# First expert layer of a four-layer graph network: settling and router joined by chunks, rows stored by node and gathered by a place-to-node table

## The chip, the cores and the metric

The kernel runs on one core of a Trainium2 chip. The metric is the device time of one execution in microseconds (us). The engines are PE (TensorE), DVE (VectorE), ACT (ScalarE), POOL (GpSimd) and SP (SyncE, which here only issues DMA transfers). Each engine runs its own list of instructions in order, and engines wait for one another through semaphores.

## The reference, cut to what matters

N = 6250 nodes of D = 256 features pass four layers, each added to its input. The change lies in the second one and in the last step of the first.

```
x = x + _L0_gnn_ref(_layernorm(x), ...)     # softmax-weighted sum over incoming edges, 8 heads of 32
x = x + _L0_ffn_ref(_layernorm(x)[None], ...)[0]   # the first expert layer, below
x = x + _L1_gnn_ref(_layernorm(x), ...)
x = x + _L1_ffn_ref(_layernorm(x)[None], ...)[0]

def _L0_ffn_ref(x, router_w, router_b, W1, b1, W2, b2):   # E = 32 experts, H = 64
    logits = xf @ router_w.T + router_b
    idx = jnp.argmax(logits, axis=-1)                # one expert for each node
    h = relu(xf @ W1[idx] + b1[idx])
    out = relu(h @ W2[idx] + b2[idx])
```

## The kernel before

The nodes lie in NT = 49 tiles of P = 128 lanes (the last has TAIL = 106). `k.acc` holds 264 words per node in SBUF (256 features and 8 denominators), and `k.x` is its first 256 words. The stages run one after the other, and at the end of each all engines meet in a barrier and its semaphores are cleared. The names in the profile are stage and tile (`settle_x`, `moe_logits`); `nodes_acc` is `k.acc`.

- `attend0` sums the edges of the first layer. POOL issues 880 gathers (L788). SP beside it writes blanks into two tables in HBM, one pair of transfers in each of the first 49 steps (`clear`, L802): `xs0` ("sorted0", rows of the first expert layer by place) and `xs1` (of the last layer).
- `settle` divides each node's sum by its denominator (`finish`, L1149, DVE), adds the layer's input x, which SP loads in chunks of 7 tiles (L1126), on POOL (L1139), and takes DVE's statistics of the sum (L1153), all 49 tiles in a row.
- `moe0` first makes mean and 1/deviation of all 49 tiles at once (L271 to L286), and then runs the router: for each tile DVE normalises it (L228), PE transposes it (L236), ACT copies it from PSUM (L265), PE multiplies it by the router's weights (L1422), DVE adds the bias (L1383). Two buffers turn, and each engine waits for the next.
- `Route.vector` then works on [128 x 49 x 32] arrays on DVE (with 8 wide products on PE, L1281 and L1282): the best expert, and from running counts each node's **place**, so that the nodes of one expert lie together and each expert's block begins at a multiple of 128. There are 80 tiles of places.
- `send` (L1394, DVE) normalises each tile again and POOL scatters its 128 rows into `xs0` at their places by an indirect DMA (L1318), with four buffers `xi`. When all have landed, the expert loop runs.
- The expert loop takes four tiles of places a round, 20 rounds. POOL loads the next four tiles of `xs0` (L1325) when PE has transposed the ones before them (L1435); PE multiplies by W1 (L1444), DVE adds b1 (L1403), PE transposes (L1452), ACT applies relu (L1365), PE multiplies by W2 (L1457), DVE adds b2 (L1407), ACT applies relu (L1368), SP stores the tile in `ys0` (L1343). In PE's order the four transposes of round i+1 stand between the W1 products and the hidden transposes of round i.
- `attend1` gathers the results back by node (L1496). Its loop already works by chunks of 7 tiles: DVE adds (L1560), takes statistics (L1564) and normalises (L1580) in turn, with mean and 1/deviation made for one chunk at a time (L271 to L286 on 7 columns).

## Time and profile before

| | |
|---|---|
| median of 3 runs | 3166.9 us (3164.47 to 3168.32) |
| the profiled execution | 3159.72 us, its span 3158.1 us |
| PE busy | 2201.9 us (70%) |
| DVE busy | 1782.5 us (56%) |
| POOL busy | 1590.8 us (50%) |
| ACT busy | 1326.0 us (42%) |
| granted TensorE clock, mean | 0.806 |

The spans in the rows are those of the profiled execution. Times in rows are from the start of its span. In a row of the timeline the first number is the start, the second how long the piece lasts, x how many instructions it holds, and the bracket how long the engine sat idle before it and what released it. PEclk is the granted TensorE clock: 0.50 is 1.2 GHz and 1.00 is 2.4 GHz.

### The profile page before, as it was taken

How to read it: one execution, taken by the hardware profiler on the slowest of the kernel's cores; microseconds unless marked ns; L12 is line 12 of the kernel's file. 1: busy time of each engine (PE TensorE's matmuls, PEld its weight loads, DVE VectorE, ACT ScalarE, POOL GpSimd, SP SyncE). 2: the span in 40 equal slices, each digit the busy share in tenths (PEclk: the TensorE clock that was granted, in tenths of full speed). 3: DMA queues.
4: the chain of work that ended last, by engine and by line, in shares of the span. 5: the costliest groups of instructions: out<-in, count | busy, mean ns of one | idle time of the engine just before them, and what ended most of it. 6: DMA issues, size and time to landing. Idle time of an engine off the chain costs nothing. (4 is left out here: it accounts for less than half of the span.)

```text
span 3158.1 us, 49641 instructions
## 1 busy us (share of the span) xinstructions
PE 2201.9 (70%) x13093; PEld 1863.9 (59%) x13094; DVE 1782.5 (56%) x4090; ACT 1326.0 (42%) x2973; POOL 1590.8 (50%) x1585
## 2 busy tenths in 40 slices
PE   7999966777777777777628069620700099999998
PEld 6888855565666555565517057410700088888887
DVE  2411026777777777776585524656753456556564
ACT  3444445555655555565402025310211444444443
POOL 0047337777777777777450443657047033333433
PEclk8999977888888888887765569765555599999999
DMA  6456466777765555555724135632212622222331
GB/s 187 152 194 232 186 220 200 210 211 205 213 178 144 145 145 143 143 145 131 73 83 119 53 118 176 144 66 51 83 61 101 235 42 47 49 47 45 48 50 24
DMA packets 213447, 402.41 MB, mean 127 GB/s; under 512 B 46139, under 2 KB 141096, under 8 KB 206639
## 3 DMA queue, kind: packets, MB, share of 16 engines
q0 software_dynamic: 84864, 206.63, 27.9%
q1 hardware_dynamic: 127278, 193.40, 18.8%
q8 instruction: 59, 0.97, 0.1%
q10 hardware_dynamic: 1168, 0.79, 0.1%
q14 instruction: 78, 0.63, 0.1%
HBM read 247.26 MB, written 155.68 MB: 128 GB/s over the span
## 5 line engine op out<-in xcount | busy, mean ns | idle before, releaser
L788 POOL DMA_INDIRECT sum_ring<-h_tab,gnn_edge_row x880 | 840.3, 955 | 267.9 <-issue 260.6
L1049 PE MATMUL sum_bank<-sum_ring,sum_one_hot 128*128 128x264 f32 x1760 | 580.7, 494 | 208.8 <-issue 191.7
L1049 PEld LDWEIGHTS sum_bank<-sum_ring,sum_one_hot 128*128 128x128 f32 x1760 | 418.1, 247 | 327.1 <-issue 222.5
L1875 POOL DMA_INDIRECT out_dram<-moe_y,moe_to_node x112 | 186.6, 1666 | 383.1 <-ACT moe_y L1901 352.1
L699 PE MATMUL rows_bank<-rows_w_rows,rows_xnT 128*128 128x264 f32 x1568 | 363.0, 391 | 6.8 <-ACT rows_h_rows L495 6.7
L699 PEld LDWEIGHTS rows_bank<-rows_w_rows,rows_xnT 128*128 128x128 f32 x1568 | 298.1, 193 | 56.7 <-ACT rows_h_rows L495 7.6
L838 ACT ACTIVATE sum_distance_by_lane<-all_iota,gnn_minus_local 128x128 bf16<-128x128 f32 x880 | 267.4, 386 | 0.1
L904 DVE TENSOR_TENSOR sum_ring<-sum_ring,sum_bank 128x1024 f32<-128x1024 f32 x220 | 265.7, 1209 | 0.4 <-ACT sum_ring L852 0.4
L1038 PEld LDWEIGHTS sum_bank<-gnn_dst_half,sum_one_hot_T 128*128 128x128 f32 x1760 | 229.9, 208 | 42.8 <-issue 39.3
L1038 PE MATMUL sum_bank<-gnn_dst_half,sum_one_hot_T 128*128 x1760 | 235.0, 292 | 27.1 <-ACT sum_one_hot_T L831 14.4
L2033 PE MATMUL moe_bank<-moe_w_low,moe_hidden_high 128*128 x896 | 244.4, 273 | 0.0
L2033 PE MATMUL moe_bank<-moe_w_high,moe_hidden_low 128*128 x896 | 244.3, 273 | 0.0
L2033 PE MATMUL moe_bank<-moe_w_high,moe_hidden_high 128*128 x896 | 244.3, 273 | 0.0
L495 ACT ACTIVATE rows_h_rows<-rows_bank 128x264 f32<-128x264 f32 x392 | 152.3, 390 | 210.2 <-PE rows_bank L699 195.9
L911 DVE TENSOR_TENSOR nodes_acc<-sum_bank,nodes_acc 128x264 f32 x440 | 188.2, 428 | 50.5 <-PE sum_bank L1049 20.1
L1917 ACT ACTIVATE moe_hidden<-moe_bank,moe_b_T 128x256 f32<-128x256 f32 x456 | 186.2, 475 | 39.5 <-PE moe_bank L2023 21.6
L843 ACT ACTIVATE sum_one_hot<-sum_distance_by_lane,all_ones 128x1024 f32<-128x1024 bf16 x110 | 126.3, 1149 | 142.8 <-PE sum_bank L1049 140.9
L596 DVE COPY gnn_dst_half<-rows_bank 128x64 f32<-128x64 f32 x49 | 11.0, 225 | 295.6 <-PE rows_bank L704 295.6
L2023 PE MATMUL moe_bank<-moe_x_high,moe_w_high 128*128 128x256 f16 x912 | 174.9, 274 | 1.7 <-DVE moe_x_low L1967 1.7
L894 DVE TENSOR_TENSOR sum_score<-sum_dst_part,sum_ring 128x64 f32<-128x64 f32 x110 | 24.8, 226 | 267.5 <-DMA sum_ring<-h_tab,gnn_edge_row 266.9
L2023 PE MATMUL moe_bank<-moe_x_low,moe_w_high 128*128 128x256 f16 x912 | 175.0, 274 | 0.0
L2023 PE MATMUL moe_bank<-moe_x_high,moe_w_low 128*128 128x256 f16 x912 | 174.9, 274 | 0.0
(408 smaller groups left out, 4164.2 us busy)
## 6 DMA issues: line engine op xcount, KB each, us to landing
h_tab<-rows_h_rows SPq DMA_DIRECT2D x49, 1056.0 KB, 3.9
sum_local_rows<-local_tab SPq DMA_DIRECT2D x110, 256.0 KB, 3.8
sorted<-sum_blank_row SPq DMA_DIRECT2D x49, 387.0 KB
moe_stage<-in_L_ffn_W_dram SPq DMA_DIRECT2D x16, 1024.0 KB
moe_tile<-sorted POOLq DMA_DIRECT2D x58, 258.0 KB, 4.2
sum_ring<-h_tab,gnn_edge_row POOLq DMA_INDIRECT x880, 3.8
sorted<-sum_zero SPq DMA_DIRECT2D x49, 256.0 KB
mask_tab<-rows_masks POOLq DMA_DIRECT2D x7, 1560.0 KB, 7.2
```

Of the source, the lines that this page charges most:

```text
L495: nc.scalar.activation(hb[:, t % 2, r, :], bank[2 + r % 4][:, 0:W0], ACT.Copy).then_inc(h_ok.sem, 1)
L699: last = nc.tensor.matmul(bank[2 + r % 4][:, 0:W0], norm.xT[:, u, c * P:(c + 1) * P], wx[:, c, r, :], start=(c == 0), stop=(c == DC - 1))
L788: nc.gpsimd.indirect_dma_start(ring[:, t % (RING * ST), :], None, k.h_tab, bass.IndirectOffsetOnAxis(k.edge_row[:, t:t + 1], 0)).then_inc( ...
L838: last = nc.scalar.activation(off[:, u * P:(u + 1) * P], k.iota[:, :], ACT.Abs, bias=k.minus_local[:, m * ST + u:m * ST + u + 1])
L904: nc.vector.tensor_tensor(to, to, by, ALU.mult).then_inc(msg_ok, 1)
L911: nc.vector.tensor_tensor(col(k.acc, b), sum_b[g % SG][:, 0:W0], col(k.acc, b), ALU.add).then_inc(added, 1)
L1038: last = nc.tensor.matmul(pick_b[n % 2][:, u * R * H0:(u + 1) * R * H0], hotT[:, n % 2, u, :], col(k.dst_half, b[u // G]), start=True, sto ...
L1049: last = nc.tensor.matmul(sum_b[j][:, 0:W0], hot[:, m % 2, t, :], ring[:, m % RING * ST + t, :], start=(u == 0), stop=(u == G - 1))
L1875: nc.gpsimd.indirect_dma_start(a["out"], bass.IndirectOffsetOnAxis(to_node[:, n % 2, h:h + 1], 0), y[:, n % 2, h, :], None, bounds_check=N ...
L1917: last = nc.scalar.activation(hg[:, q, m * B1:(m + 1) * B1], bank[q][:, m * B1:(m + 1) * B1], ACT.Gelu, scale=1.0 / (XS * WS), bias=col(b1 ...
L2023: last = nc.tensor.matmul(bank[q][:, m * B1:(m + 1) * B1], w1[pw][:, c, bass.ds(e * F1 + (2 * q + m) * P, P)], xh[px][:, u, c, :], start=( ...
L2033: last = nc.tensor.matmul(bank[6 + u][:, h * D:(h + 1) * D], hh[ph][:, u, m, h * P:(h + 1) * P], w2[pw][:, m, bass.ds(e * D, D)], start=(m ...
```

## The change

`settle` is gone as a stage. `moe0` begins with a loop over 7 chunks of 7 tiles: while a chunk is normalised and goes through the router, DVE and POOL finish the next chunk and take its statistics, and mean and 1/deviation are made for 7 columns. x is loaded four chunks ahead, into the tile that later holds b2. The normalised tiles lie in a ring of XN = 8, from which PE transposes them and SP stores them by node in a table in HBM, `xn0` ("normal0"), whose first 128 rows are zero. The weights are loaded by ACT's queue (router, W1, b1) and SP's (W2 in the third chunk, b2 after the last addition).

There is no second normalisation and no scatter. After the places are known, `slots` builds on DVE, for four node tiles at a time, two one-hot arrays: `hot_lane` (is the node's place in this lane of its tile of places) and `hot_tile` (is it in this tile of places, times the node's row number in `xn0`). PE adds their 49 products in one PSUM bank, which makes the table `slot_rows`: for each of 84 tiles of places and each lane the row of `xn0` that lies there, 0 (a zero row) where the place is empty. POOL then gathers the 84 tiles of the expert loop by that table, where it loaded them in one piece before. In `attend0` the blanks for `xs0` are no longer written.

```diff
 def attend0(nc, a, k):
...
             def clear(t):
-                for (tab, m), empty, w in zip(k.sorted, (zero, blank), (D, XW)):
+                for (tab, m), empty, w in zip(k.sorted, (blank,), (XW,)):
...
             sp.wait_ge(zero_ok, 4)
+            sp.dma_start(k.xn0[0:P, :], zero[:, :]).then_inc(zeroed, 16)
...
-def settle(nc, a, k):
...
+    def slots(self, v, ch):
...
+        for b, step in enumerate(self.steps):
+            if b >= 2:
+                v.wait_ge(self.hot_used, b - 1)
+            m, q0 = len(step), step[0]
+            nc.vector.tensor_tensor(self.hot_lane[:, b % 2, 0:m, :], self.k.iota[:, :].rearrange("p (o l) -> p o l", o=1).broadcast_to([P, m, P]),
+                                    self.lane[:, q0:q0 + m].rearrange("p (m o) -> p m o", o=1).broadcast_to([P, m, P]), ALU.is_equal)
+            for q in step:
+                last = nc.vector.tensor_scalar(self.hot_tile[:, b % 2, q - q0, :], self.starts[:, :], self.first[:, q:q + 1], self.code[:, q:q + 1], ALU.is_equal, ALU.mult)
+            last.then_inc(self.hot_ok, 1)
+        v.wait_ge(self.hot_used, len(self.steps))
+        nc.vector.tensor_scalar(self.rows[:, :], self.bank[0][:, 0:self.starts.shape[1]], 0.25, None, ALU.add).then_inc(self.rows_ok, 1)
...
+    def slot_rows(self, pe):
...
+                last = self.nc.tensor.matmul(self.bank[0][:, 0:self.starts.shape[1]], self.hot_lane[:, b % 2, q - step[0], :], self.hot_tile[:, b % 2, q - step[0], :],
+                                             start=(q == 0), stop=(q == n - 1))
...
 def moe0(nc, a, k):
...
         def _(pool):
             route.pool()
-
             for t in range(NT):
-                u, m = t % 4, P if t < NT - 1 else TAIL
-                pool.wait_ge(row_ok, t + 1)
-                nc.gpsimd.indirect_dma_start(k.xs0, bass.IndirectOffsetOnAxis(k.rows0[0:m, t:t + 1], 0), xi[0:m, u, :], None).then_inc(scattered[u], 16)
...
+                nc.gpsimd.tensor_tensor(k.x[:, t, :], k.x[:, t, :], x[:, n % AHEAD, u, :], ALU.add).then_inc(node_ok, 1)
+            all_written(pool)
+            pool.wait_ge(route.rows_ok, 1)
+            for n in range(T + 4):
+                x_ps.slot(pool, n)
+                nc.gpsimd.indirect_dma_start(xi[:, n % 4, :], None, k.xn0, bass.IndirectOffsetOnAxis(tile_rows[:, n:n + 1], 0)).then_inc(tile_in[n % 4], 16)
...
         def _(sp):
...
+            for c in range(CHUNKS):
+                if c + AHEAD < CHUNKS:
+                    sp.wait_ge(node_ok, (c + 1) * CH)
+                    load_x(c + AHEAD)
+                if c == 2:
+                    sp.dma_start(w2[:, :, :], a["L0_ffn_W2"].rearrange("e h d -> h e d")).then_inc(loaded_b, 16)
+                for t in range(c * CH, (c + 1) * CH):
+                    sp.wait_ge(xn_ok, t + 1)
+                    sp.dma_start(k.xn0[(t + 1) * P:(t + 2) * P, :], xn[:, t % XN, :]).then_inc(written[t % XN], 16)
+            sp.wait_ge(node_ok, NT)
...
         def _(v):
...
+            def normalise(t):
+                if t >= XN:
+                    v.wait_ge(t_ps, t - XN + 1)
+                    v.wait_ge(written[t % XN], 16 * (t // XN))
...
+            for c in range(CHUNKS):
...
+                if more:
+                    finish(t1 + LEAD)
+                    stats(t1)
+                scales(c)
+                for j in range(CH):
+                    normalise(t0 + j)
+                    if more and j + 1 < CH:
+                        finish(t1 + j + 1 + LEAD)
+                        stats(t1 + j + 1)
+                    if j == 2 and c:
+                        logits(c - 1)
+                if more:
+                    variance(c + 1)
+            route.codes(v, ch)
...
             route.vector(v, ch)
+            route.slots(v, ch)
...
-            def send(i, u):
...
-            rounds(v, NT, 4, send)
```

On POOL the order around the first expert layer reads as follows, before (-) and after (+); `sorted` is `xs0`, `normal` is `xn0`, `moe_b` in the addition is the b2 tile that holds x.

```order
-L1133 MEMSET settle_x 128x256
-L1139 TENSOR_TENSOR nodes_acc<-nodes_acc,settle_x 128x256 x49
-L112 UNCONDITIONAL_BRANCH
-L115 ISA
-L1311 UNCONDITIONAL_BRANCH
-L1211 IOTA moe_tile_row_i 1x80
-L1318 DMA sorted<-moe_tile,nodes_rows 12544x256 x49
...
+L1155 IOTA moe_tile_row_i 1x80
+L1331 TENSOR_TENSOR nodes_acc<-nodes_acc,moe_b 128x256 x49
+L1336 DMA moe_tiles<-normal,moe_slot_rows 128x256 x84
```

The 49 scatters are gone, and the loads of the loop (one direct transfer for each tile) have become 84 gathers.

On DVE the end of one chunk and the start of the next read in the changed kernel as follows (`moe_work` holds the denominators, `moe_tiles` the ring of normalised tiles).

```order
L1435 TENSOR_SCALAR moe_tiles<-nodes_acc,moe_mean,moe_rstd 128x256
L271 TENSOR_TENSOR moe_tmp<-nodes_stats 128x7
L272 TENSOR_SCALAR moe_mean<-moe_tmp 128x7
...
L277 SCALAR_TENSOR_TENSOR moe_var<-moe_var,moe_tmp 128x7
L1414 TENSOR_TENSOR nodes_acc<-nodes_acc,moe_work 128x256
L1418 BN_STATS nodes_stats<-nodes_acc 128x6
L282 RECIPROCAL moe_rstd<-moe_sd 128x7
...
L286 TENSOR_TENSOR moe_rstd<-moe_rstd,moe_tmp 128x7
L1435 TENSOR_SCALAR moe_tiles<-nodes_acc,moe_mean,moe_rstd 128x256
L1414 TENSOR_TENSOR nodes_acc<-nodes_acc,moe_work 128x256
```

The settling of the next chunk now stands between the normalisations of this one, where it was a stage of its own.

On DVE the end of the places reads in the changed kernel as follows; `moe_total` and `moe_running` are the memory of `hot_lane` and `hot_tile`.

```order
L1217 CAST moe_expert<-moe_expert_f 1x80
L1254 CAST moe_place_i<-moe_place 128x49
L1255 TENSOR_SCALAR moe_place_i<-moe_place_i 128x49
L1256 CAST moe_tile_of<-moe_place_i 128x49
L1259 TENSOR_TENSOR moe_lane_of<-moe_place,moe_tile_of 128x49
L1264 TENSOR_TENSOR moe_total<-all_iota,moe_lane_of 128x512
L1267 TENSOR_SCALAR moe_running<-moe_tile_starts,moe_tile_of,moe_row_code 128x84 x4
...
L1270 TENSOR_SCALAR moe_slot_rows<-moe_bank 128x84
L1473 CAST nodes_rows<-moe_place 128x49
```

The pair L1264, L1267 stands there 13 times (the last time for one tile); before, the cast to `nodes_rows` came straight after `moe_expert`, and then 49 normalisations for the scatter.

## Rows read from the trace of the kernel before
**Rows 1.** Stretch: busy (x) of PE, PEld, DVE, ACT, POOL; PEclk, DMA share, GB/s

```profile
1606.40:1655.10 48.70, 0.00 (x0) 0.00 (x0) 44.90 (x100) 0.01 (x1) 41.43 (x50) 0.53 0.42 132
1655.10:1725.40 70.30, 63.19 (x296) 59.48 (x296) 33.10 (x113) 20.28 (x51) 0.18 (x1) 0.50 0.52 135
1725.40:1773.20 47.80, 7.08 (x16) 3.75 (x16) 38.98 (x38) 0.00 (x0) 0.00 (x0) 0.57 0.00 0
1773.20:1842.20 69.00, 0.00 (x0) 0.00 (x0) 19.99 (x49) 0.00 (x0) 48.08 (x49) 0.50 0.26 93
1842.20:1978.30 136.10, 119.38 (x728) 101.25 (x728) 49.91 (x160) 71.42 (x244) 45.22 (x84) 0.88 0.51 158
```

**Rows 2.** Timeline of the stretch of settle, POOL and DVE

```profile
1612.00 35.94 POOL L1139 TENSOR_TENSOR nodes_acc<-nodes_acc,settle_x 128x256 f32<-128x256 f32 x42 [5.27 <-DMA settle_x<-in_x_dram]
...
1616.54 0.60 DVE L1149 TENSOR_TENSOR nodes_acc<-nodes_acc,settle_denominator 128x256 f32<-128x256 f32 x1
...
1617.40 0.60 DVE L1149 TENSOR_TENSOR nodes_acc<-nodes_acc,settle_denominator 128x256 f32<-128x256 f32 x1
```

**Rows 3.** Timeline of DVE in the router loop, and its end

```profile
1717.42 0.41 DVE L228 TENSOR_SCALAR moe_y<-nodes_acc,moe_mean,moe_rstd 128x256 f32 x1 [0.43 <-PE moe_bank L236]
...
1720.06 0.41 DVE L228 TENSOR_SCALAR moe_y<-nodes_acc,moe_mean,moe_rstd 128x256 f32 x1 [0.43 <-PE moe_bank L236]
...
1725.14 0.19 DVE L1383 TENSOR_TENSOR moe_logits<-moe_bank,moe_router_bias 128x32 f32<-128x32 f32 x1 [0.66 <-PE moe_bank L1422]
```

**Rows 4.** Timeline of DVE where the places are made, wide array, end

```profile
1727.41 1.79 DVE L1222 TENSOR_TENSOR moe_work<-moe_logits,moe_best 128x1568 f32<-128x1568 f32 x1
...
1772.93 0.19 DVE L1387 CAST nodes_rows<-moe_place 128x49 int32<-128x49 f32 x1
```

**Rows 5.** Timeline of POOL and PE at the loop's first loads

```profile
1842.24 2.59 POOL L1325 DMA_DIRECT2D moe_tile<-sorted  x4 [5.56 <-DMA sorted<-moe_tile,nodes_rows]
...
1844.52 2.82 PE L1435 MATMUL moe_bank<-all_ident,moe_tile 128*128 128x128 f32 x8 [101.18 <-DMA moe_tile<-sorted]
```

**Rows 6.** Timeline of DVE in attend1, the start of a chunk

```profile
2019.38 0.20 DVE L282 RECIPROCAL gnn_rstd<-gnn_sd 128x7 f32<-128x7 f32 x1 [1.06 <-ACT gnn_sd L1529]
...
2020.68 0.41 DVE L1580 TENSOR_SCALAR gnn_xn<-nodes_acc,gnn_mean,gnn_rstd 128x256 f32<-128x256 f32 x1
2021.01 0.42 DVE L1560 TENSOR_TENSOR nodes_acc<-nodes_acc,gnn_expert_rows 128x256 f32<-128x256 f32 x1
```

**Rows 7.** Timeline of ACT in attend1, the square root that opens each chunk

```profile
2008.27 0.20 ACT L1529 ACTIVATE gnn_sd<-gnn_var 128x7 f32<-128x7 f32 x1
2019.14 0.20 ACT L1529 ACTIVATE gnn_sd<-gnn_var 128x7 f32<-128x7 f32 x1
2031.91 0.20 ACT L1529 ACTIVATE gnn_sd<-gnn_var 128x7 f32<-128x7 f32 x1
```

**Rows 8.** Timeline of the expert loop: transposes of two rounds, loads between

```profile
1882.98 1.04 PE L1435 MATMUL moe_bank<-all_ident,moe_tile 128*128 128x128 f32 x8
...
1884.02 2.55 POOL L1325 DMA_DIRECT2D moe_tile<-sorted  x4 [3.21 <-PE moe_bank L1435]
...
1888.73 1.04 PE L1435 MATMUL moe_bank<-all_ident,moe_tile 128*128 128x128 f32 x8
```

**Rows 9.** Landing times by the DMA view, in KB each and us

```profile
moe_tile<-sorted POOLq DMA_DIRECT2D x84, 128.0 KB, 2.4
...
gnn_expert_rows<-results,nodes_rows POOLq DMA_INDIRECT x49, 3.8
```

**Rows 10.** Landing of attend0's 880 gathers (L788), from the view of their line

```profile
DMA to landing us min/median/max: 2.7/3.8/5.8
```

**Rows 11.** As rows 1: attend0 while blanks are written, and later

```profile
800.00:900.00 100.00, 76.74 (x344) 60.87 (x345) 76.10 (x157) 54.44 (x109) 75.63 (x81) 0.81 0.70 202
1000.00:1100.00 100.00, 77.85 (x360) 61.56 (x360) 75.48 (x156) 56.40 (x111) 75.75 (x80) 0.83 0.52 144
```

**Rows 12.** As rows 1: the expert loop in its first 27 us

```profile
1845.00:1872.00 27.00, 26.69 (x101) 22.26 (x101) 6.09 (x20) 9.94 (x30) 6.45 (x12) 0.50 0.35 107
```

More of the change, by code:

```diff
@@ L1283, in tensor, with slots_in @@
         last.then_inc(self.counted, 1)
+    def slots_in(self, s, tiles, hot_lane, hot_tile, rows):
+        n = self.top * NT
+        self.lane, self.first, self.code = (s.sb(x, [P, n]) for x in ("lane_of", "tile_of", "row_code"))
+        self.place_i, self.starts = s.sb("place_i", [P, n], I32), s.sb("tile_starts", [P, tiles])
+        self.hot_lane, self.hot_tile, self.rows = hot_lane, hot_tile, rows
+        self.hot_ok, self.hot_used, self.rows_ok = s.sem("slots_ready"), s.sem("slots_used"), s.sem("slot_rows_ready")
+        self.steps = [range(q, min(q + 4, n)) for q in range(0, n, 4)]
@@ L1309, in moe0, with all_written @@
         block = s.block()
+        def all_written(eng):
+            for u in range(XN):
+                eng.wait_ge(written[u], 16 * ((NT - u + XN - 1) // XN))
         @block.gpsimd
@@ L1348, in _ @@
         def _(act):
-            norm.root(act)
-            tiles(act, NT, 2, lambda t, u: norm.keep(act, t, u, lg_ps))
+            act.dma_start(rw_n[:, :], a["L0_ffn_router_w"]).then_inc(router, 16)
+            act.dma_start(rb[:, :], a["L0_ffn_router_b"].rearrange("(o e) -> o e", o=1).broadcast_to([P, E0])).then_inc(router, 16)
+            for c in range(DC):
+                act.dma_start(w1[:, c, :, :], a["L0_ffn_W1"][:, c * P:(c + 1) * P, :].rearrange("e p h -> p e h")).then_inc(loaded, 16)
+            v = a["L0_ffn_b1"].rearrange("e h -> (e h)").rearrange("(o n) -> o n", o=1)
+            act.dma_start(flat(b1[:, :, :]), v.broadcast_to([P, v.shape[1]])).then_inc(loaded, 16)
+            for c in range(CHUNKS):
+                part = slice(c * CH, (c + 1) * CH)
+                act.wait_ge(var_ok, c + 1)
+                nc.scalar.activation(sd[:, part], var[:, part], ACT.Sqrt).then_inc(sd_ok, 1)
+                for t in range(c * CH, (c + 1) * CH):
+                    act.wait_ge(t_ps, t + 1)
+                    if t >= 2:
+                        act.wait_ge(lg_ps, t - 1)
+                    nc.scalar.activation(xnT[:, t % 2, :], bank[t % 2][:, 0:D], ACT.Copy).then_inc(t_ok, 1)
             act.wait_ge(route_ok, 1)
```

218 lines of the change are left out of this document (122 added, 96 removed).

## The prediction

> **What bounds the kernel now.** I read the busy times by stretch first, because the shares of the whole span mix stages. From the end of attend0 at 1606.4 to the start of attend1 at 1978.3 no engine is the bound of the whole; one after the other is [rows 1]. In settle POOL and DVE are both busy and PE stands still for 48.7 us. In the router loop PE is (63.2 of 70.3 us, at the lower clock, 0.50). Making the places is a chain on DVE, 47.8 us. In the 69.0 us of the scatter PE does nothing at all and POOL issues 49 transfers. In the expert loop PE is the bound again (119.4 of 136.1 us). The stretches follow one another, so a microsecond taken from any of them is one off the time, unless the next one gives it back.
>
> The timelines then give the pace. In settle DVE's pair of division and statistics repeats every 0.86 us (1616.54 to 1617.40), and so do POOL's additions (42 in 35.94 us) [rows 2]. Two tiles of the router take 2.64 us, 1.32 each, and its last logits come at 1725.3 [rows 3]. The places end at 1773.1 [rows 4]; PE's first transpose of the expert loop starts at 1844.5 [rows 5]: 71.4 us between them.
>
> **Joined loop, -22 us.** Before: 1606.4 to 1725.3, 118.9 us. After, in steps:
> - Head. The first addition starts at 1612.0, as before, since it waits for the first chunk of x [rows 2]. Seven tiles at 0.86 us, then statistics: 1618.5. Moments are 7 small operations at about 0.20 us, the duration of such a one [rows 6]: 1.4. One pair (0.86), the router's copy (0.2), and the five steps to 1/deviation, 1.3 us in attend1 (2019.38 to 2020.68) [rows 6]. First normalisation at 1622.3.
> - One chunk. Seven pairs at 0.86, seven normalisations at 0.33 (the pace 2020.68 to 2021.01) [rows 2, 6], 1.4 and 1.3 for the small ones, 0.3 for logits: 11.3 us. attend1, which has the same form, takes 10.9 and 12.8 us a chunk (2008.27, 2019.14, 2031.91) [rows 7]. I take 11.6, near the sum: attend1's POOL issues gathers where this one adds. Six chunks: 1691.9.
> - Last chunk. Nothing is settled beside it, so PE bounds it: seven tiles at 1.32 [rows 3] and two more of such turns until the first is through, 12 at most; I take 11.3. Logits at 1703.2.
> That is 96.8 us against 118.9. Bounds: 11.3 a chunk gives 2 us more; 12.8 takes 7. A first chunk of x that comes late, since four chunks and ACT's weight loads start with it, costs up to 5.
>
> What hides here: PE needs 7 x 1.32 = 9.2 us a chunk, under 11.3. SP's stores of the ring (128 KB each) are waited for eight tiles later, some 12 us, against a landing of 2.4 us for such a size [rows 9]; W2 issued in the third chunk delays them, up to 3 us. The loads of x, the weights and the stores are about 18 MB in 97 us, 185 GB/s, which attend0 moves (202) [rows 11]. The 4 MB of b2 leave after the last addition and have some 75 us of places and table; at 202 GB/s they take 20. The small operations of `codes` lie under PE's last chunk.
>
> The trace shows DVE and POOL in each other's way: the division takes 0.60 us in settle [rows 2], a two-input operation of the same size 0.42 where POOL only gathers [rows 6]. By the Trainium skill ("SBUF — State Buffer", Who interferes with whom) VectorE and GpSimd share a port pair: a VectorE operation with two SBUF inputs contends with GpSimd's reads, and one in a 2-port mode blocks it. By that rule the normalisation, a tensor-scalar operation, could take part too and would hold POOL's additions up. The row has it at 0.41 us for 256 columns, like the two-input one, so it runs in no such mode here; I leave it at 0.33 in the sum and keep the other case as a rival.
>
> **Places, 0.** The same instructions stand there, with the same 8 products.
>
> **Table instead of scatter, -47 us.** Before, 71.4 us from the places to PE's first transpose [rows 4, 5]. After:
> - Four small operations, 0.8 us.
> - 12 full steps and one single. On DVE one of 512 columns and four of 84. A wide operation of 1568 columns takes 1.79 [rows 4], so 512 take 0.6; one of 49 columns takes 0.19 [rows 4], and without a wait behind it at least 0.13, so four of them take 0.5 to 0.8. On PE four products, which the router does in 1.32 at the lower clock (two of 128 and two of 32 columns) [rows 3]. The buffers are doubled, so the slower counts: 1.4 a step, 17 us. The bounds are 1.1 a step (13.5 us) and 2.0 (24.5 us), if the handing over is not hidden.
> - Emptying PSUM and waking POOL, 1.3 us. Table ready at 19 us; bounds 15.5 and 27.
> - The first gather lands. No row shows one from `xn0`; gathers of rows of about this size take 2.7 at least and 3.8 in the median [rows 9, 10], a direct load started at 1842.24 feeds PE at 1844.52 [rows 5]. I take 3.3 with the wait.
> - Gathers leave POOL every 1.25 us (80 in 100 us) [rows 11] where four loads take 2.59 [rows 5]: the fourth tile is 1.7 us later.
> 24.0 us against 71.4.
>
> **Expert loop, +11 us.** A round is 5.75 us at the full clock (1882.98 to 1888.73), its transposes take 1.04, and POOL's first load starts 1.04 after the first of them [rows 8]. POOL's fourth gather starts 1.04 + 3 x 1.25 = 4.8 us after the transposes' start and lands at 4.8 + L; it is due at 5.75 + 0.78 = 6.5. What is missing, L - 1.7, is shared by two rounds, because a round that stalls also starts the next later: (L - 1.7)/2 a round. With L = 2.7 that is 0.5, with 3.8 it is 1.05. Loads in this very loop land in 2.4 [rows 9], 0.1 above the idle one, so I take L = 3.0, 0.65 a round. About 17 of the 20 rounds run at the full clock; in the first 27 us only three do, at 0.50 [rows 12], and there nothing is missing. Together 11 us, bounds 8 and 18. Behind the stalled transposes PE's hidden transposes and W2 products queue, and DVE, ACT and SP behind these, so all of it is on the path. By the Trainium skill ("DMA: Bandwidth & Descriptors", Anatomy of one DMA) such a transfer takes 2.0 us and its bytes at 436 GB/s, 2.3 us for 128 KB; the loop would then lose 5 us and not 11. No row has a gather that fast.
>
> **attend0, 0.** 49 transfers of 256 KB less. But POOL issues 80 or 81 gathers in 100 us while blanks are written and 80 afterwards, at 202 and 144 GB/s [rows 11]: the issue is the bound, and DMA was hidden. Price 0; a few fewer late landings could give 2.
>
> **Sum.** -22 - 47.4 + 11 = -58.4. The profiled execution took 3159.7 us (span 3158.1), which is 7.2 below the median of the runs, 3166.9. 3159.7 - 58.4 = 3101.3 for an execution like it, and **3108 us** on the scale of the medians. Less than 0.2% (6 us) can't be told from no change here.
>
> **The rivals.**
> 1. *POOL bounds the expert loop* (0.15). The gathers land like attend0's slowest, 5.8 us [rows 10], because 42% of their rows are the one zero row (4502 empty of 10752) and all read the same address. (5.8 - 1.7)/2 = 2.05 a round, 35 us: 3132. For it: POOL would be busy 5.0 of 5.75 us. Against: the median of 3.8.
> 2. *The joined loop is paced by the shared port or by DMA* (0.12). If each normalisation costs 0.2 more and each addition holds DVE up, a chunk takes 13.5 to 14 us: +13, 3121. For it: the 0.60 against 0.42. This is the skill's rule on ports from above, in a milder form.
> 3. *PE's clock is up when the loop starts* (0.11). Before, PE stood still for 101 us ahead of it and ran 27 us at 0.50; now it works through the table's products until some 5 us before. Three rounds at 5.75 in place of 9 give 10: 3098; with the last chunk at the higher clock too, 3094.
> 4. *Slower* (0.02). The table and the gathers would have to lose the 69 us won. That is a landing of gathers of L = (69/17) x 2 + 1.7 = 9.8 us, far above the largest of 5.8. With L = 10.5 it is 75 us lost: 3173.
> 5. *Nothing gained* (0.01): the loop waits for something else that is late, b2 above all, until the old time. It would have to land 50 us after my estimate.
>
> **How the numbers follow.** The likeliest case has 0.59, with its own range 3096 to 3122 (head and chunks +12 or -2, table +8 or -4, loop +7 or -3, not all at once). The range over the cases, 3092 to 3134, leaves out rival 4 and the far ends, some 2 in 10 with what I have not thought of. Faster: all but rivals 4 and 5 and a margin, 0.95; same 0.02; slower 0.03.
>
> **What the profile will show.** The last logits 97 us after the end of attend0, with chunks of 11 to 12 us, divisions at 0.5 to 0.6; 13 steps at 1.4 us; the first gather some 68 us after the last logits; rounds of 6.2 to 6.6 us at the full clock with PE's transposes waiting for the fourth gather, POOL almost without idle time; the pace of attend0 unchanged. I would be wrong through the chunk (waits of DVE on stores or on the square root), through the step of the table, or through a landing time unlike 3 us.

## Result and profile after the change

The changed kernel takes 3144.6 us in the median of nine runs (3132.8 to 3158.1); the kernel before took 3166.9 in the runs beside them (3152.5 to 3168.3). The ratio is 0.994, with a 95% interval of 0.9925 to 0.9956: 0.6% faster. The forecast was 3108 with a range of 3092 to 3134; the sign was right and the size was not. The profiled execution has a span of 3141.1 us, 17.0 less than before, where 58.4 were forecast. One execution of e7 (3562.6 us) and one of e17 (3270.9 us) were over 1.5% above the fastest of their kernel and are left out of its median and ratio.

The stretches of the stage in the changed kernel (columns as in [rows 1]; in order: the head, the joined loop to its last normalisation, the router's last tiles, the places, the table, the expert loop):

```profile
1606.40:1630.40 24.00, 0.42 (x2) 0.28 (x2) 14.13 (x34) 2.06 (x4) 8.81 (x12) 0.56 1.01 267
1630.40:1706.60 76.20, 58.12 (x261) 53.15 (x261) 65.61 (x206) 17.99 (x50) 27.51 (x38) 0.50 0.54 147
1706.60:1714.00 7.40, 6.90 (x35) 6.76 (x35) 1.94 (x8) 1.92 (x5) 0.00 (x0) 0.50 0.93 366
1714.00:1761.90 47.90, 7.37 (x16) 3.90 (x16) 38.85 (x38) 0.00 (x0) 0.00 (x0) 0.57 0.10 44
1761.90:1788.50 26.60, 22.68 (x98) 21.35 (x98) 21.09 (x68) 0.00 (x0) 0.00 (x0) 0.50 0.00 0
1791.30:1960.90 169.60, 145.04 (x728) 119.81 (x728) 50.52 (x160) 75.26 (x244) 77.36 (x83) 0.75 0.51 126
```

attend0 ends where it did (1606.3, before 1606.4), though it moves less (153 GB/s over its length instead of 164): its term of 0 was right. The last logits come at 1714.0 instead of 1703.2, and the places take 47.9 us as before. PE's first transpose starts 29.4 us after the places (forecast 22.3, before 71.4). The expert loop takes 169.6 us with a mean clock of 0.75, where [rows 1] has 0.88 over the old one. From first transpose to the start of attend1 it was 133.8 before, so the loop gives 35.8 us back and not 12.7 (11 for its rounds and 1.7 for the spacing of its first gathers).

**The head.** ACT at the stage's start:

```profile
1607.57 0.88 ACTq L1374 DMA_DIRECT2D moe_w<-in_L_ffn_W_dram  x1
1608.48 0.40 ACT L1374 MOVE_SHAPE moe_w<-in_L_ffn_W_dram  x1 [0.94 <-issue]
1608.91 10.04 ACTq L1374 DMA_DIRECT2D moe_w<-in_L_ffn_W_dram  x1
1618.98 8.83 ACTq L1376 DMA_DIRECT2D moe_b<-in_L_ffn_b_dram  x1
1627.84 1.28 ACT L1380 ACT_TABLE_LOAD   x1 [18.96 <-issue]
1629.13 0.21 ACT L1380 ACTIVATE moe_sd<-moe_var 128x7 f32<-128x7 f32 x1
```

The second half of W1 and b1 hold ACT for 10.0 and 8.8 us each: this is the issue of a DMA, not its landing. The square root that the first chunk needs, with its table load of 1.3 us, stands behind them. DVE had the variances at 1620.8 and soon idled for 7.4 us, until the square root was done at 1629.3; the first normalisation starts at 1630.4, not 1622.3.

**The chunks** are 11.55 us apart (1630.42, 1641.97, 1653.54, 1665.08), as forecast, but of other parts. DVE in the fourth:

```profile
1665.08 0.41 DVE L1435 TENSOR_SCALAR moe_tiles<-nodes_acc,moe_mean,moe_rstd 128x256 f32<-128x256 f32 x1
1665.40 0.42 DVE L1414 TENSOR_TENSOR nodes_acc<-nodes_acc,moe_work 128x256 f32<-128x256 f32 x1
1665.74 0.42 DVE L1418 BATCH_NORM_STATS2 nodes_stats<-nodes_acc 128x6 f32<-128x256 f32 x1
1672.16 0.41 DVE L1435 TENSOR_SCALAR moe_tiles<-nodes_acc,moe_mean,moe_rstd 128x256 f32<-128x256 f32 x1 [6.00 <-DMA normal<-moe_tiles]
...
1673.16 0.70 DVE L1435 TENSOR_SCALAR moe_tiles<-nodes_acc,moe_mean,moe_rstd 128x256 f32<-128x256 f32 x1
```

The division takes 0.42 and not 0.60, the normalisation mostly 0.69 and not 0.41: POOL's addition now runs beside the normalisation, where in [rows 2] it ran beside the division. And once DVE waits 6.0 us for a store of the ring: this store was issued at 1654.0, behind W2 (1652.45), and took 18.1 us to land where the median is 1.8.

**The table.** DVE's wide comparison of two steps in turn, 3.72 us apart, 1.86 a step against the 1.4 forecast:

```profile
1766.54 0.69 DVE L1264 TENSOR_TENSOR moe_total<-all_iota,moe_lane_of 128x512 f32<-128x512 f32 x1 [0.56 <-PE moe_bank L1278]
1767.15 1.02 DVE L1267 TENSOR_SCALAR moe_running<-moe_tile_starts,moe_tile_of,moe_row_code 128x84 f32<-128x84 f32 x4
...
1770.26 0.69 DVE L1264 TENSOR_TENSOR moe_total<-all_iota,moe_lane_of 128x512 f32<-128x512 f32 x1 [0.39 <-PE moe_bank L1278]
```

DVE has some 1.6 us of work in a step (1.54 in e17 below, where it does not wait) and then waits for PE. PE at the lower clock, first in the table and then in the router of the kernel before:

```profile
1764.49 7.95 PE L1278 MATMUL moe_bank<-moe_running,moe_total 128*128 128x84 f32 x33 [32.20 <-DVE moe_running L1267]
```

```profile
1716.45 0.67 PE L236 MATMUL moe_bank<-all_ident,moe_y 128*128 128x128 f32 x2
1716.91 0.90 PE L1422 MATMUL moe_bank<-moe_router,moe_y 128*128 128x32 f32 x4
```

A product is two instructions on PE, a transpose is one. So a step of the table has eight, 98 in all for the 49 products, and a tile of the router has six.

**The expert loop.** PE in two rounds, and the landing of the 84 gathers from the view of their line:

```profile
1821.05 2.00 PE L1541 MATMUL moe_bank<-moe_w,moe_tiles 128*128 x16
1822.88 0.93 PE L1532 MATMUL moe_bank<-all_ident,moe_tiles 128*128 128x128 f32 x6
1825.11 0.41 PE L1532 MATMUL moe_bank<-all_ident,moe_tiles 128*128 128x128 f32 x2 [1.29 <-DMA moe_tiles<-normal,moe_slot_rows]
...
1828.76 3.67 PE L1541 MATMUL moe_bank<-moe_w,moe_tiles 128*128 x16
1832.23 1.91 PE L1532 MATMUL moe_bank<-all_ident,moe_tiles 128*128 128x128 f32 x8
```

```profile
DMA to landing us min/median/max: 2.7/3.4/6.3
```

PE waits for the fourth gather, as forecast. What was not forecast is the next round: W1's products take 3.67 us instead of 2.00, the clock is at 0.50. That comes back six times. The same 728 instructions keep PE busy 145.0 us, 25.6 more than before, and this is most of the 35.8; only 10 us are longer stands.

### The profile page after: what moved, and what is told of

It is laid out like the page before. It is cut to its first block and busy times, and to the rows that moved or that the text cites. A ratio compares the mean times of both kernels' runs of the same rounds, so it can differ in the third digit from the quotient of the medians.

```text
span 3141.1 us, 48982 instructions
## 1 busy us (share of the span) xinstructions
PE 2252.2 (72%) x13191; PEld 1907.5 (61%) x13192; DVE 1791.8 (57%) x4143; ACT 1331.6 (42%) x2981; POOL 1570.9 (50%) x1535
## 5 line engine op out<-in xcount | busy, mean ns | idle before, releaser
L788 POOL DMA_INDIRECT sum_ring<-h_tab,gnn_edge_row x880 | 838.6, 953 | 268.0 <-issue 259.4
L912 DVE TENSOR_TENSOR nodes_acc<-sum_bank,nodes_acc 128x264 f32 x440 | 188.5, 428 | 56.2 <-PE sum_bank L1050 26.6
```

The costliest lines, as they stand in the source:

```text
L788: nc.gpsimd.indirect_dma_start(ring[:, t % (RING * ST), :], None, k.h_tab, bass.IndirectOffsetOnAxis(k.edge_row[:, t:t + 1], 0)).then_inc( ...
L912: nc.vector.tensor_tensor(col(k.acc, b), sum_b[g % SG][:, 0:W0], col(k.acc, b), ALU.add).then_inc(added, 1)
```

## Experiments

Each group ran on a chip of its own, with the kernel before beside it. On the chips of the first four groups the kernel before takes 3494 to 3571 us instead of 3164 to 3167. Nearly all of the difference lies in attend0 (its 100 us from 800 hold 64 gathers in the trace of the second group where [rows 11] have 81). So I compare ratios within a group, and stages by their traces. All times from the stage's start, in us; the loop is from PE's first transpose to the start of attend1. The ratio is that of the timed runs to the kernel before in the same group (a 95% interval of 0.002 to 0.007 to either side); where there is none, the kernel ran once, for its trace.

| run | group | last logits | first transpose | loop | attend1 starts | clock in loop | ratio |
|---|---|---|---|---|---|---|---|
| before | | 118.9 | 238.1 | 133.8 | 371.9 | 0.88 | |
| changed | | 107.7 | 185.0 | 169.6 | 354.6 | 0.75 | 0.994 |
| c1, c2 (changed again) | 2, 3 | 108.4, 108.2 | 185.7, 185.2 | 171.8, 175.4 | 357.5, 360.6 | 0.74, 0.70 | 0.989, 0.994 |
| e3 weights late | 1 | 94.4 | 172.1 | 163.0 | 335.1 | 0.80 | 0.988 |
| e4 eight tiles | 1 | 109.0 | 185.6 | 161.6 | 347.2 | 0.76 | 0.988 |
| e5 direct loads | 1 | 106.8 | 184.0 | 138.5 | 322.5 | 0.85 | |
| e6 fill | 1 | 107.9 | 185.2 | 172.3 | 357.5 | 0.84 | 0.991 |
| e7 spread | 2 | 108.1 | 185.7 | 147.5 | 333.2 | 0.89 | 0.984 |
| e8, e12 all | 2, 3 | 94.4, 94.4 | 171.5, 171.4 | 164.9, 157.8 | 336.4, 329.2 | 0.74, 0.77 | 0.985, 0.986 |
| e9 stall | 2 | 108.1 | 184.8 | 132.5 | 317.3 | 0.90 | |
| e13, e14 stalls | 4 | 107.4, 107.9 | 184.4, 184.5 | 139.6, 162.4 | 324.0, 346.9 | 0.88, 0.73 | |
| e15 node order | 4 | 107.6 | 185.0 | 155.0 | 340.0 | 0.83 | |
| e11 add on DVE | 3 | 114.4 | 191.7 | 171.2 | 362.9 | 0.75 | |
| e10, e18 late and spread | 3, 5 | 94.5, 94.4 | 172.2, 171.7 | 152.6, 148.0 | 324.8, 319.7 | 0.82, 0.86 | 0.981, 0.982 |
| e16, e17 warm | 4, 5 | 94.3, 94.4 | 169.5, 169.4 | 140.6, 137.4 | 310.1, 306.8 | 0.96, 0.96 | 0.985, 0.978 |

The changed kernel was not run in groups 1, 4 and 5. In group 2 the times alone do not tell e7 (0.979 to 0.988) from the changed kernel (c1, 0.985 to 0.992); there, and for e3, the gain is read from the traces.

### The weights' place (e3)

My theory was that the issue of W1 and W2 holds up whoever issues next on that queue; the rival, that the chunks of x fill the queues anyway.

```diff
 # ACT
-            for c in range(DC):
-                act.dma_start(w1[:, c, :, :], ...).then_inc(loaded, 16)
-            act.dma_start(flat(b1[:, :, :]), ...).then_inc(loaded, 16)
             for c in range(CHUNKS):
...
+            for c in range(DC):
+                act.dma_start(w1[:, c, :, :], ...).then_inc(loaded, 16)
+            act.dma_start(flat(b1[:, :, :]), ...).then_inc(loaded, 16)
             act.wait_ge(route_ok, 1)
 # SP
-                if c == 2:
-                    sp.dma_start(w2[:, :, :], ...).then_inc(loaded_b, 16)
...
             sp.wait_ge(node_ok, NT)
+            sp.dma_start(w2[:, :, :], ...).then_inc(loaded_b, 16)
```

> W1 and b1 are issued by ACT after its last copy of the router loop, W2 by SP after the last addition, ahead of b2. Theory A (a full DMA queue holds up whoever issues into it: ACT's square root behind W1 and b1, DVE's normalisation behind the stores that SP could not start after W2): the first normalisation comes at 1622.3 instead of 1630.4, the wait of 6.0 us on a store is gone, chunks stay at 11.55, the last logits come near 1700 instead of 1714, and the time falls by 14 us. Rival B (the four chunks of x and the stores fill the queues by themselves): the first normalisation stays near 1630 or the 6 us reappear elsewhere, the time falls by under 4. Rival C: the 9 MB of weights then land after the table is ready and the loop starts late: the loop's first transpose stays near 1791.

The first normalisation comes at 16.5 instead of 24.1, the last logits at 94.4 instead of 107.7, and the loop's first transpose 12.9 us earlier, so the weights, 5 MB of them moved and 9 MB in all, land in time behind the places and the table. DVE's waits over the joined loop, in the changed kernel and then in this one:

```profile
DVE moe_rstd L282 <- ACT moe_sd L1380: 9.0, 2, 7.4
DVE moe_tiles L1435 <- DMA normal<-moe_tiles: 6.0, 1, 6.0
DVE moe_logits L1439 <- PE moe_bank L1512: 5.1, 1, 5.1
```

```profile
DVE moe_logits L1438 <- PE moe_bank L1511: 5.2, 1, 5.2
DVE moe_rstd L282 <- ACT moe_sd L1375: 1.6, 1, 1.6
```

Both waits are gone and nothing took their place. That the issues held up the square root and the store is shown; theory A's sum of 14 us was 13.3. Its picture of a full queue is not: here the issue of W1's second half takes 20.9 us, with no chunk of x under way but behind W2 and b2, and nothing that the stage waits for stands behind it.

### What the loop waits for (e5, e7, e15)

e5 replaces the gathers by direct loads of the same table in node order (the tiles are then not sorted by expert):

```diff
-nc.gpsimd.indirect_dma_start(xi[:, n % 4, :], None, k.xn0, bass.IndirectOffsetOnAxis(tile_rows[:, n:n + 1], 0))
+pool.dma_start(xi[:, n % 4, :], rows(k.xn0, (n % NT + 1) * P, P))
```

> The 84 gathers of the expert loop are direct loads of 128 rows of the same table in node order (so the tiles are not sorted by expert; everything else is done). Theory A (the gathers are what the loop lost by): rounds of 5.75 us with the clock at 1.00 after some 27 us, loop 133 to 138 us instead of 169.6, time 32 to 36 less. Rival B (the loop is slow by what is around it, weights or stores): the loop stays over 160.

At the full clock 14 of its 16 rounds take 5.75 or 5.76 us, and PE never waits for a tile after the first ones. So the gathers are what the loop lost by; the changed kernel itself takes 171.8 and 175.4 on chips of this kind. e7 keeps them and changes which row an empty place reads:

```diff
-nc.vector.tensor_scalar(self.rows[:, :], self.bank[0][...], 0.25, None, ALU.add)
+nc.vector.tensor_scalar(self.rows[:, :], self.bank[0][...], 0.25, self.k.col[:, 0:1], ALU.add, ALU.max)
```

Empty places hold 0, and nodes' rows start at 128, so the maximum with the lane's number sends lane p of an empty place to zero row p.

> Empty places are coded with the lane instead of 0, so that they read 128 different zero rows and not all the same one; nothing else differs. If the one hot row makes gathers slow (the first rival of the prediction), the gathers land earlier by over 0.5 us in the median and the loop falls from 170 to 150 or less. If it does not, landings stay near 3.4 us and the loop stays within 5 us of the changed kernel's in the same group.

The loop took 147.5 us against 171.8 for the changed kernel in the same group, 24.3 less, and PE's waits for gathers are 9.7 us in all against 18.8. Once the clock is up it stays up to the loop's end, as it does in e10 and e18, which have this edit too. Of the landing I had no reading on that chip; the fifth group has one, in e18:

```profile
L1336 POOL DMA_INDIRECT moe_tiles<-normal,moe_slot_rows x84: 940/946/964, 1770.9 to 1910.5; - x84
...
DMA to landing us min/median/max: 2.8/3.1/3.2
```

The largest is 3.2 us, where it was 6.3, and the median 3.1 against 3.4. The one zero row was what made gathers late. e15 gathers by a table in node order, with no empty places at all (again unsorted tiles):

> The loop still gathers, by indirect DMA, but the table holds the rows in node order (row 128 x tile + lane, none empty, none twice in a tile), so the tiles are not sorted. If the hot zero row is the whole reason why gathers land late, the waits on gathers are those of the run with spread zero rows (0.5 us a round) and the loop takes 145 to 150. If the scattered order of rows costs time too, waits are shorter than that, 0 to 0.3 a round. If neither, the loop stays near 170.

PE's waits for gathers are 8.9 us in all, near e7's 9.7, and its rounds 6.3 to 6.8 as e7's 6.3 to 6.8. So the order in which the rows lie costs nothing that shows. Its loop is longer than e7's (155.0) because it begins with four rounds at 0.50 where e7 has two.

### Why the clock falls (e6, e9, e13, e14)

Count a round from the start of W1's products to the next, and as stand all the time in it in which PE does nothing. In the five traces of the four-buffer loop with one zero row (changed, c1, c2, e3, e11), 16 rounds have 2 us or more of stand. All 16 have a fall to 0.50 in them. Below 2 us it goes either way: the first trace has three falls in rounds with 1.3, 1.7 and 1.8 us of stand, and the largest stand without a fall is 1.7 (c1). That is a correlation, so I made stands of known size on direct loads. The edit is the direct load of e5, and ahead of the fourth load of every fourth round:

```diff
+                if n % 16 == 15:
+                    pool.wait_ge(spare_ok, n // 16)
+                    nc.gpsimd.tensor_tensor(spare[:, 0:1024], mask[:, 0:1024], mask[:, 0:1024], ALU.add).then_inc(spare_ok, 1)
                 pool.dma_start(xi[:, n % 4, :], ...)
```

> Direct loads in node order as in the earlier run (tiles not sorted), and in every fourth round one addition of 1024 columns on POOL ahead of the fourth load, which makes this load some 1 to 2 us late for PE; five such stalls in the loop. Theory A (a stall of this length brings the granted clock to 0.50): each stall is followed by a round at 0.50, which costs 2 to 4 us beyond the stall itself, the loop takes 152 to 168 us instead of 138.5. Rival B (the clock is not brought down by stalls): only the stalls are added, 5 to 8 us, the loop takes 144 to 147 us and the clock stays at 1.00 between them.

The addition took 1.9 us and the stand was only 0.4: too short to be a test. The clock did not fall with it, and the loop (132.5) was shorter than e5's by luck: its clock was up 9 us after the loop's start, e5's after 37, and no run gives a reason for that. So the doses were raised.

> As the run with a stall (direct loads in node order, tiles not sorted; POOL adds ahead of the fourth load in every fourth round), but the addition has 1536 columns in place of 1024, 2.85 us instead of 1.90, so that PE should stand some 1.4 us instead of 0.4, five times. If stalls of that length bring the clock down, each is followed by a round at 0.50 and the loop takes 150 to 160 us against 132.5 to 138.5; if not, it takes 138 to 145.

> The same with two additions of 1024 columns, 3.8 us, so that PE should stand some 2.3 us, five times. In the runs of the changed kernel nearly every round with 1.7 us or more of stand at the full clock had a fall to 0.50 in it. If the stand is the cause, all five stalls do that and the loop takes 158 to 168 us; if the falls come by themselves, the stalls cost 2.3 us each and the loop takes 144 to 150.

With stands of 0.9 to 1.2 us (1.3 to 1.6 in the whole round, where an undisturbed one has 0.5) a fall came in one round of five, and the loop took 139.6. With 1.9 to 2.1 us (2.3 to 2.5 in all) all three that met the full clock brought a fall; the other two met a clock that was down already. The loop took 162.4. The first of the three:

```profile
2172.52 2.00 PE L1546 MATMUL moe_bank<-moe_w,moe_tiles 128*128 x16
2174.36 0.82 PE L1537 MATMUL moe_bank<-all_ident,moe_tiles 128*128 128x128 f32 x6
2177.11 0.41 PE L1537 MATMUL moe_bank<-all_ident,moe_tiles 128*128 128x128 f32 x2 [1.93 <-DMA moe_tiles<-normal]
...
2178.33 3.29 PE L1559 MATMUL moe_bank<-moe_w,moe_hidden_T 64*128 x8 [0.37 <-ACT moe_hidden_T L1405]
2181.55 3.67 PE L1546 MATMUL moe_bank<-moe_w,moe_tiles 128*128 x16
```

A stand of 1.93 us, with 0.37 more behind it, and then three whole rounds and parts of two at 0.50: these five rounds take 46.8 us and not 28.8. That stands of this size bring the clock down in this loop is shown. That they are the only cause is not: e5, e9, e13 and e14 have one fall each with no such stand ahead of it, and c1 and c2 one each with 0.5 and 0.9 us.

e6 tried the reverse, work for PE in place of the stand: six transposes into a bank that is overwritten, ahead of the wait for the fourth gather.

```diff
+                    if u == 3:
+                        for r in range(6):
+                            nc.tensor.transpose(bank[7][:, D:D + P], k.ident[:, :], k.ident[:, :])
                     turn(i + 1, u)
```

> Work is added: six more transposes of 128 columns on PE in each round, ahead of the wait for the fourth gather (120 in all, 0.13 us each at the full clock, 0.27 at half; their result is overwritten). Theory A (the stand of PE brings the clock down): PE works where it stood, the clock stays at 1.00 after the first rounds, rounds take 6.2 to 6.8, and the loop is shorter than 169.6 in spite of the added work: about 140 to 150, time 20 to 30 less. Rival B (the clock falls for another reason): the loop gets longer by 5 to 25 us.

The mean clock is 0.84, where the changed kernel has 0.70 to 0.75, but the loop took 172.3, as long as there (169.6 to 175.4): the 120 transposes cost what the clock gave. Neither theory's numbers came. It is no clean test either: the clock still falls five times in the loop, and the added work brings new stands of up to 1.5 us ahead of W2's products.

### More buffers (e4, e8, e12)

Four more tile buffers in memory that is dead by then (`route.pick`), PE's loop unrolled to two rounds, and POOL waiting for the tile eight places back:

```diff
+        xb = flat(route.pick[0][:, :, :])[:, 0:4 * D].rearrange("p (u f) -> p u f", u=4)
+        xi = [xa[:, u, :] for u in range(4)] + [xb[:, u, :] for u in range(4)]
...
-                x_ps.slot(pool, n)
+                if n >= 8:
+                    pool.wait_ge(x_ps.sem, n - 3)
```

> The expert loop has eight tile buffers instead of four, so that POOL gathers one round further ahead. Theory A (late fourth gathers make PE stand still for 0.3 to 1.3 us, and each such stand is followed by a round at a granted clock of 0.50): PE never waits for a gather after the first rounds, the clock stays at 1.00 after some 27 us, rounds take 5.75, the loop takes 133 to 138 us instead of 169.6 and the time falls by 32 to 36. Rival B (the clock falls for another reason, or POOL's 5.0 us a round are the bound): the waits of about 22 us go, but slow rounds at 0.50 remain; the loop takes 150 to 160 and the time falls by 10 to 20.

The waits for gathers went (5.6 us in all, the first tiles), as both theories said, and the loop is 161.6: rival B. e8 adds late weights and spread rows, and e12 is e8 again.

> W1, b1 and W2 late as in the run with the weights late, eight tile buffers as in the run with eight tiles, and empty places read 128 different zero rows instead of one. Theory A (stalls on gathers bring the clock down): the loop's first transpose comes 172 us after the stage's start and on an undisturbed chip the loop takes 133 to 140 us, the time is 45 to 50 us under the changed kernel. Rival B (with deeper gathers something else stalls PE, as DVE's waits on stores in the run with eight tiles): the loop stays near 160, the time is 20 to 25 us under it.

> The kernel with all three edits (weights late, eight tile buffers, spread zero rows) once more, to see if its loop of 164.9 us, with two long stretches at the lower clock and no stall ahead of them, comes again. If such stretches come by chance, the loop takes 140 to 150 us this time; if eight buffers bring them, it stays at 160 to 168.

164.9 and 157.8. In all three the clock falls two to four times, with at most 0.8 us of stand in the round of the fall and in the one ahead of it. From e12:

```profile
2096.67 1.05 PE L1534 MATMUL moe_bank<-all_ident,moe_tiles 128*128 128x128 f32 x8
2097.64 0.98 PE L1552 MATMUL moe_bank<-all_ident,moe_hidden 128*128 128x128 f32 x4
2099.13 1.99 PE L1557 MATMUL moe_bank<-moe_w,moe_hidden_T 64*128 x8 [0.51 <-issue]
2101.05 3.50 PE L1544 MATMUL moe_bank<-moe_w,moe_tiles 128*128 x16
```

What does differ from e5 is that the hidden transposes are stretched (0.98 us, in e5 0.60), since DVE begins its additions 2.6 us after the start of W1's products, not 1.2. Why the clock falls there stays open, and eight buffers were not run on a chip like the first and the last.

### The port (e11)

The additions of x made by DVE, not POOL:

```diff
-                nc.gpsimd.tensor_tensor(k.x[:, t, :], k.x[:, t, :], x[:, n % AHEAD, u, :], ALU.add).then_inc(node_ok, 1)
...
+                nc.vector.tensor_tensor(k.x[:, t, :], k.x[:, t, :], x[:, n % AHEAD, u, :], ALU.add).then_inc(node_ok, 1)
```

> The 49 additions of x are made by DVE instead of POOL. If POOL's additions are what makes DVE's normalisation take 0.69 us instead of 0.41 in the changed kernel (a shared port), all 49 normalisations now take 0.41, at a pace of 0.33, and a chunk takes 7 x 4 x 0.34 + 3.0 = 12.5 us instead of 11.55. If the 0.69 has another cause (the stores that read the ring, PE's reads), it stays and a chunk takes 14 us or more.

DVE's 49 normalisations, in the changed kernel and in this one (ns, least/median/most):

```profile
L1435 DVE TENSOR_SCALAR moe_tiles<-nodes_acc,moe_mean,moe_rstd x49: 390/692/764, 1630.4 to 1706.3; 128x256 f32<-128x256 f32 x49
```

```profile
L1434 DVE TENSOR_SCALAR moe_tiles<-nodes_acc,moe_mean,moe_rstd x49: 396/398/413, 1909.4 to 1991.7; 128x256 f32<-128x256 f32 x49
```

POOL's addition is the cause of the 0.69. That is the rule of the Trainium skill ("SBUF — State Buffer", Who interferes with whom) which the prediction set aside; the trace agrees with it in that the normalisation is long beside POOL's addition and short without it. Whether it runs in a 2-port mode, the trace does not show. Without POOL the joined loop is still 6.2 us longer than c2's, about 1 us for each of six chunks, since DVE has a fourth operation per tile.

### Versions (e10, e16, e17, e18), and the references

> The changed kernel once more, as the reference of this group, because the chip of the first group ran the kernel before in 3559 us instead of 3167. Every theory expects the stages of the first result: 107.7 us to the last logits, the loop's first transpose at 185, and a loop of 170 us with the clock falling to 0.50 several times; on a chip like that of the first group also delays of DVE and ACT while gathers run, which the first result does not show.

> The changed kernel, as the reference of this group. Every theory expects 107.7 us to the last logits, the loop's first transpose at 185 and a loop of 168 to 173 us.

The ratios to the kernel before are 0.9888 (0.9851 to 0.9924) and 0.9935 (0.9914 to 0.9955).

> W1, b1 and W2 late, and empty places spread over the 128 zero rows, four tile buffers as in the changed kernel. If the two causes found so far (the DMA queues ahead of ACT's square root and of DVE's ring, 14 us; the hot zero row, 24 us) are independent, the loop's first transpose comes at 172, the loop takes 145 to 150 us, and the time is 35 to 40 us under the changed kernel's in the same group. If the loop of the spread run was short by luck of the clock, the loop is over 160.

3421.5 us against 3473.1 for c2: 51.6 less, a ratio to before of 0.9805 (0.9776 to 0.9834). In the traces the stage is 35.8 us shorter (324.8 against 360.6), as expected. The traced executions differ outside it too, by 18.8 us ahead of the stage and by 11 behind it, where the kernels are the same; so not all of the 51.6 is shown to be the edits' work. e16 is this kernel with work for PE ahead of the loop:

```diff
 # slot_rows, in each step
+            for r in range(2):
+                self.nc.tensor.transpose(self.bank[7][:, 256:384], self.k.ident[:, :], self.k.ident[:, :])
 # ahead of the first turn
+            for r in range(24):
+                nc.tensor.transpose(bank[7][:, D:D + P], k.ident[:, :], k.ident[:, :])
```

> The best kernel so far (weights late, zero rows spread), and PE given work in the wait ahead of the loop: two transposes of 128 columns more in each of the table's 13 steps, and 24 more before the first gather has landed (results overwritten). If PE's clock at the start of the loop follows what PE did before, the first three to four rounds of 9.9 us take 6.3 instead and the time falls by a further 10 to 16 us, to 0.976 to 0.978 of the kernel before. If the clock rises no sooner, the time stays at 0.98.

The clock came up in the table, fell for 7 us in the loop's first round, behind stands for the first gathers, and is at 1.00 from the second round on. The ratio, 0.9852 (0.9803 to 0.9902), was too wide to tell it from e10, so the two ran side by side:

> The kernel with late weights, spread zero rows and added work for PE ahead of the loop, beside the same one without the added work. If the clock that is up at the start of the loop is worth its 12 us (loop 140.6 us against 152.6 in the traces of two groups), this one is 0.3 to 0.4% faster than the other in the same group, at 0.977 of the kernel before. If the work added makes the clock fall later in the loop, both are equal.

> The kernel with late weights and spread zero rows, as the partner of the one with added work: 0.980 of the kernel before as in its first group, with three to four rounds of 9.9 us at the start of the loop and a loop of 150 to 155 us.

e17 takes 3093.1 us, 0.9778 of before (0.9760 to 0.9795), e18 3106.0, 0.9816 (0.9796 to 0.9836); the kernel before took 3164.3. The loop of e18, then that of e17:

```profile
1773.70:1921.70 148.00, 126.96 (x728) 104.59 (x728) 50.24 (x160) 73.82 (x244) 77.23 (x83) 0.86 0.47 145
```

```profile
1782.00:1919.40 137.40, 113.21 (x728) 93.32 (x728) 49.96 (x160) 72.77 (x244) 77.01 (x82) 0.96 0.50 155
```

The same 728 instructions take 113.2 us where they took 127.0. In e18 the clock is at 0.50 for the loop's first 39.5 us and then does not fall again. In e17 it is up from 1762.3, falls once, at 1786.2, behind four stands of 0.4 to 0.8 us for the first gathers, is back at 1793.0 and stays up. And the step of the table shrinks from 1.86 to 1.54 us, DVE's own work, since PE's products now run at the full clock for most of it. e17 is the fastest kernel here: 2.2% under the kernel before, against 0.6% for the change as made.

## Why the prediction was wrong, step by step

The terms, as times of the stage; "repaired" is e18, which differs from the changed kernel in two things, where the weights are issued and which zero row an empty place reads.

| term | forecast | changed | repaired |
|---|---|---|---|
| joined loop | -22.0 | -11.2 | -24.5 |
| places | 0 | +0.1 | 0 |
| table and first gather | -49.1 | -42.0 | -41.9 |
| expert loop (with 1.7 of spacing) | +12.7 | +35.8 | +14.2 |
| attend0 | 0 | -0.1 | |
| sum | -58.4 | -17.4 | -52.2 |

- **Head (8.1 us short).** The step that failed: "First normalisation at 1622.3". The landing of x was weighed ("costs up to 5"), and x did land as before. What I did not cost is that the issue itself holds the engine: ACT 18.9 us, with the square root behind it. I asked what stands behind a wait and not what stands behind an issue. e3 shows it. The trace of before had the sign of it, in SP's issues of W1 and W2 at the start of `moe0`, where nothing stood behind them:

```profile
1656.07 4.81 SPq L1334 DMA_DIRECT2D moe_w<-in_L_ffn_W_dram  x2
1660.93 4.87 SPq L1335 DMA_DIRECT2D moe_w<-in_L_ffn_W_dram  x1
```

- **Chunks (right in sum by luck, wrong in parts) and W2.** 11.55 against 11.6. The pair of division and statistics fell from 0.86 to 0.67, and the normalisation rose from 0.33 to 0.62: POOL's addition lengthens whichever of the two it meets. The duration of 0.41 where POOL only gathers could not show that the normalisation is immune, because that row had no POOL addition beside it; e11 shows it. Rival 2 was priced from this and its mechanism is real, but its chunk of 13.5 to 14 did not come, since what the division gave paid for it. "W2 ... delays them, up to 3 us" measured 6.0; a last chunk of 9.9 instead of 11.3 and smaller differences took back 3.2.
- **Places and attend0.** Right, with the work that hides the blanks (POOL's issue) as named.
- **Table (7.1 short).** The step was mis-sized: 1.86 us and not 1.4. DVE's part is 1.54 (the four operations of 84 columns take 0.94 in it, above my 0.5 to 0.8), and a step of PE at the lower clock takes 1.86, not 1.32. I read it off the router as four products of 128 and 32 columns. But two of those four are transposes, one instruction each, and a product is two: six instructions there and eight here, which at 0.50 follow one another about every 0.21 us with 32 columns as with 84; the rest of the 1.86 is handing over. That is 5.5 us over twelve steps; the end of the table and the first gather took another 1.6.
- **Expert loop (23.1 short, the largest miss).** The step that failed is one landing time for every gather and rounds "at the full clock" whatever PE waits. "I take L = 3.0, 0.65 a round" was right for a gather without the hot row: e18 has 3.1 and rounds of 6.2 to 6.4, and its loop is 1.5 us off the forecast. Rival 1 named the hot row, and I gave it 0.15 because the median of attend0's gathers, which have no such row, speaks against it; those rows could not bear on it. The rival also had the wrong form: not every gather at 5.8, but a median of 3.4 with a tail to 6.3. What the tail then does was in no case of mine: rounds with 2 us and more of stand, after which the clock is down for a round or more. Against e18 that is 18.1 us of longer PE work and 3.5 of stands. I took the clock as low at the loop's start and up from there on, as in the 0.88 before, while e14 shows that stands bring it down again.
- **Rival 3** (clock up at the start) did not come by itself: PE worked 22.7 of the table's 26.6 us and stayed at 0.50. e17 shows that it can be had, and that it is worth 13.0 us in the timed runs and 10.6 us of the loop in the traces.

The range missed because the three misses were all on one side. The table was a misread row. The other two come from work brought together that stood apart before: weights issued ahead of the square root, and gathers, with their empty places on one row, ahead of PE's transposes.

## What to carry to other kernels

A DMA issue is an instruction of its engine: before a load is moved to another engine's queue, see what stands behind it there, and how long such loads took to issue. When a table of row numbers has a filler value, spread it over many rows; one instruction's second operand was worth 24 us of the loop here. Where PE's waits grow by one or two microseconds at the full clock, cost the slower rounds after them too: in e14 one stand of 1.9 us made five rounds 18.0 us longer. And useless work in PE's gaps ahead of a loop can pay.

## What was not expected of the hardware

- Issuing the second half of W1 (1 MB) took ACT 10.0 us and b1 8.8 us while four chunks of x were under way; the first half took 0.9. Issued late (e3) they took 20.9 and 4.5 us. SP's issue of W2 (2 MB) took 0.7. What sets the length was not tried.
- Gathers in which 42% of the rows are one and the same row land in 3.4 us in the median and 6.3 at most; with 128 different rows in its place 3.1 and 3.2 (e18, which also has the weights late).
- On the chips of groups 1 to 4 DVE began its first addition of a round 1.6 to 3.6 us after the start of W1's products in many rounds with gathers under way, but 1.2 us after it with direct loads; on the first and the last chip it was 1.2 with gathers too. The same chips are the ones with the slower attend0. The cause was not tried.
- The clock fell with no stand ahead of it only on those chips, and most often with eight tile buffers, whose cause is open.
